# The lag stage of a four-part sequence kernel: query and key projected by halves, norms from transposed pair sums, the moves between partitions behind the rotation

## What is computed

```python
q, k, v = (causal_dwconv(silu(x @ W), conv_w) for each of Wq, Wk, Wv)   # 4 taps
z, a, b = x @ Wz, x @ Wa, x @ Wb
q = q * cos + rot_half(q) * sin      # rot_half(u): u1, u2 = halves of u; [-u2, u1]
k = k * cos + rot_half(k) * sin
q = q / max(norm(q), 1e-12);  k = k / max(norm(k), 1e-12)
for s in range(4):                   # k, v and a, delayed by s positions
    out += (sum(q * lag(k, s)) / sqrt(128) * sigmoid(lag(a, s) * b)) * lag(v, s)
out = out * rms(out) * norm_w * silu(z)
return out @ Wout
```

## Time and profile before

| | us |
|---|---|
| median of 3 runs | 3301.22 (3300.37 to 3301.49) |
| the profiled execution | 3301.86 |
| its span | 3300.1 |
| TensorE busy in the span | 3091.1 (94%), granted clock 0.966 on average |
| VectorE, ScalarE, GpSimd busy | 1793.2 (54%), 1160.3 (35%), 1041.8 (32%) |
| lag stage, about | 977 to 2160 |

### The profile page before, as it was taken

How to read it: one execution, slowest core, us unless ns; L and a number is a source line. 1 busy time by engine, 2 the same in 40 slices (tenths; PEclk the granted TensorE clock), 3 DMA queues, 4 the chain that set the end, 5 groups by cost and what they waited for, 6 DMA issues and landing times. The chain is left out here.

```text
span 3300.1 us, 39332 instructions
## 1 busy us (share of the span) xinstructions
PE 3091.1 (94%) x14752; PEld 2575.3 (78%) x14752; DVE 1793.2 (54%) x2587; ACT 1160.3 (35%) x2498; POOL 1041.8 (32%) x678
## 2 busy tenths in 40 slices
PE   6886499999979999999999999959999999999997
PEld 5665388888858888888888888848888888888886
DVE  4888633333367777777777777773222222222225
ACT  4232222112125555655555656532211121112110
POOL 4556223222224333333333333222222232223221
PEclk9987699999989999999999999979999999999999
DMA  3000101000032222222222222121010001000001
GB/s 116 1 1 0 61 20 39 20 20 1 1 110 59 58 61 58 62 58 62 74 60 60 61 59 61 40 77 58 20 39 20 19 20 39 20 20 27 12 0 51
DMA packets 54318, 135.46 MB, mean 41 GB/s; under 512 B 8305, under 2 KB 8689, under 8 KB 51313
## 3 DMA queue, kind: packets, MB, share of 16 engines
q1 hardware_dynamic: 54128, 132.95, 13.4%
HBM read 90.71 MB, written 8.65 MB: 30 GB/s over the span
## 5 line engine op out<-in xcount | busy, mean ns | idle before, releaser
L530 DVE TENSOR_TENSOR experts_inner<-experts_U,experts_gated 128x512 f32<-128x512 f32 x128 | 88.5, 691 | 593.5 <-PE experts_U L46 587.9
L492 POOL TENSOR_TENSOR experts_inlo<-experts_inner,experts_inhi 128x512 fp32r<-128x512 f32 x128 | 165.4, 1293 | 754.9 <-ACT experts_inhi L460 754.9
L543 DVE SCALAR_TENSOR_TENSOR x_tok<-experts_D,expert_weight,x_tok 128x512 f32<-128x512 f32 x256 | 191.3, 750 | 148.9 <-PE experts_D L46 148.9
L1437 DVE SCALAR_TENSOR_TENSOR lag_cq<-lag_A,lag_conv,lag_cq 128x511 f32<-128x511 f32 (+2 forms) x192 | 142.8, 744 | 196.0 <-ACT lag_cq L1349 196.0
L457 ACT ACTIVATE experts_gated<-experts_G 128x512 f32<-128x512 f32 x128 | 76.5, 598 | 458.5 <-PE experts_G L46 458.5
L1412 POOL TENSOR_TENSOR lag_rot_q<-lag_cq,lag_cos_sin 128x512 f32<-128x512 f32 x64 | 83.0, 1297 | 478.9 <-DVE lag_cq L1437 478.9
L44 PE MATMUL lag_A<-xT_hi,lag_w_hi 128*128 128x512 f32 x512 | 211.5, 413 | 3.8 <-DVE lag_cq L1437 2.7
L44 PE MATMUL lag_B<-xT_hi,lag_w_hi 128*128 128x512 f32 x512 | 212.6, 415 | 0.0
L460 ACT ACTIVATE experts_inhi<-experts_inner 128x512 fp32r<-128x512 f32 x128 | 80.9, 632 | 374.5 <-DVE experts_inner L530 374.5
L44 PE MATMUL experts_G<-xT_hi,experts_whi 128*128 128x512 f32 x528 | 207.4, 393 | 0.8 <-DVE expert_weight L1079 0.8
L45 PE MATMUL experts_G<-xT_lo,experts_whi 128*128 128x512 f32 x528 | 206.9, 392 | 0.0
(11 more groups left out here) (279 smaller groups left out, 8178.4 us busy)
## 6 DMA issues: line engine op xcount, KB each, us to landing
lag_raw<-in_head_weights SPq DMA_DIRECT2D x16, 1024.0 KB, 6.2
lag_b_row<-lag_b_scratch SPq DMA_DIRECT2D x64, 256.0 KB, 3.2
lag_swapped_q<-lag_cq SPq DMA_DIRECT2D x128, 128.0 KB, 2.3
lag_swapped_k<-lag_ck SPq DMA_DIRECT2D x128, 128.0 KB, 2.3
experts_raw<-in_expert_gate SPq DMA_DIRECT2D x16, 512.0 KB, 3.7
experts_raw<-in_expert_up SPq DMA_DIRECT2D x16, 512.0 KB, 4.6
experts_raw<-in_expert_down SPq DMA_DIRECT2D x16, 512.0 KB, 5.6
x_tok<-in_x SPq DMA_DIRECT2D x4, 1024.0 KB, 5.3
```

Source lines behind the costliest of these rows:

```text
L492: pool.tensor_tensor(in_lo[t % 2][:, f, :], inner[f][:, :], f32(in_hi[t % 2][:, f, :]), ALU.subtract).then_inc(s_hlo, 1)
L530: ins = dve.tensor_tensor(inner[f][:, :], U[f][:, :], gated[f][:, :], ALU.mult)
L543: ins = dve.scalar_tensor_tensor(row, D[tt][:, :], expert_weight[:, bass.ds(e + j * EXPERTS, 1)], row, op0=ALU.mult, op1=ALU.add)
L1437: dve.scalar_tensor_tensor(out[:, shift:], src[:, 0:SEQ - shift], wj, out[:, shift:], op0=ALU.mult, op1=ALU.add).then_inc(done, 1)
```

## The change

The halves of query and key are sorted anew on the host (`by_halves`): the first matrix of a head gives channels 0 to 63 of q and 0 to 63 of k (bank A, `c1`), the second the channels 64 to 127 of both (bank B, `c2`). The convolution weights follow. The partners of the rotation then lie on the same partition of two tiles: r1 = c1 cos - c2 sin, r2 = c2 cos + c1 sin. The results are moved by four DMAs into `rot_q` and `rot_k`, where all channels of q lie on one tile and all of k on another; before, it was the inputs that were moved.

The squares of `c1` and `c2` are added on GpSimd (`pairs`), transposed by TensorE into the second bank of the `scores` tile, and summed over each half by a reduction on VectorE, which gives eight sums (query and key, alternating by tile). On TensorE the second projection moves ahead of the scores. `gain` gets a second buffer, and VectorE takes `gain` before `prob`.

```diff
         squares, pairs = sb("squares", [P, 2, SEQ]), sb("pairs", [P, SEQ])
+        gain = [sb(f"gain{p}", [P, TPB, BAND]) for p in range(2)]
+        turned = scores[:, 2:4, :].rearrange("p a n -> p (a n)")
...
@@ SyncE @@
-                        sp.wait_ge(s_cq, f.s * TAPS + TAPS)
-                        until(sp, s_rot_q, f.s)
-                        for half in range(2):
-                            to, of = half * 64, 64 - half * 64
-                            sp.dma_start(swapped_q[to:to + 64, :], cq[of:of + 64, :]).then_inc(s_swap_q, 16)
...
+                        sp.wait_ge(s_r1, f.s + 1)
+                        until(sp, s_s, f.s)
+                        sp.dma_start(rot_q[0:64, 0:SEQ], r1[0:64, :]).then_inc(s_move1, 16)
+                        sp.dma_start(rot_k[0:64, :], r1[64:128, :]).then_inc(s_move1, 16)
+                        sp.wait_ge(s_r2, f.s + 1)
+                        sp.dma_start(rot_q[64:128, 0:SEQ], r2[0:64, :]).then_inc(s_move2, 16)
+                        sp.dma_start(rot_k[64:128, :], r2[64:128, :]).then_inc(s_move2, 16)
...
@@ TensorE @@
-                        projection(f, 0, A, s_q)
+                        projection(f, 0, A, s_a1)
+                        until(pe, s_sz, f.s - 1)
+                        projection(f, 1, B, s_a2)
                     if l1:
-                        pe.wait_ge(s_rot_q, l1.s + 1)
-                        pe.wait_ge(s_rot_k, l1.s + 1)
-                        pe.wait_ge(s_n2, l1.s + 1)
+                        pe.wait_ge(s_move1, l1.s * 32 + 32)
+                        pe.wait_ge(s_move2, l1.s * 32 + 32)
+                        pe.wait_ge(s_sum, l1.s + 1)
...
-                    if f:
-                        until(pe, s_sz, f.s - 1)
-                        projection(f, 1, B, s_k)
...
-                        pe.wait_ge(s_sqr, f.s * 2 + 2)
+                        pe.wait_ge(s_pair, f.s + 1)
                         until(pe, s_prob, f.s)
-                        for n in range(2):
-                            for t in range(TPB):
-                                col = NORM_AT + n * TPB + t
-                                last = pe.matmul(scores[:, 0, col:col + 1], squares[:, n, t * P:(t + 1) * P],
-                                                 ones[:, :], start=True, stop=True)
+                        for t in range(TPB):
+                            last = pe.transpose(turned[:, t * P:(t + 1) * P], pairs[:, t * P:(t + 1) * P], ident[:, :])
...
@@ GpSimd @@
                     if f:
-                        until(pool, s_s, f.s)
-                        pool.wait_ge(s_cq, f.s * TAPS + TAPS)
-                        pool.tensor_tensor(rot_q[:, 0:SEQ], cq[:, :], cos_sin[:, 0, :], ALU.mult).then_inc(s_cos_q, 1)
+                        pool.wait_ge(s_c1, f.s * TAPS + TAPS)
+                        until(pool, s_move1, f.s * 32)
+                        pool.tensor_tensor(r1[:, :], c1[:, :], cos_sin[:, 0, :], ALU.mult).then_inc(s_cos1, 1)
...
+                        pool.tensor_tensor(r2[:, :], c2[:, :], cos_sin[:, 0, :], ALU.mult).then_inc(s_cos2, 1)
+                        pool.wait_ge(s_sqr, f.s * 2 + 2)
+                        until(pool, s_nrm, f.s)
+                        pool.tensor_tensor(pairs[:, :], squares[:, 0, :], squares[:, 1, :], ALU.add).then_inc(s_pair, 1)
...
@@ VectorE @@
+                        tap(0, f, A, c1, 1, s_c1)
+                        dve.wait_ge(s_gate, f.s + 1)
+                        until(dve, s_prob, f.s - 1)
+                        dve.scalar_tensor_tensor(gain[f.s % 2][:, :, :], gate[:, :, :], 1.0,
+                                                 band_t[:, :].unsqueeze(1).to_broadcast([P, TPB, BAND]),
+                                                 op0=ALU.add, op1=ALU.mult).then_inc(s_gain, 1)
+                        tap(0, f, A, c1, 2, s_c1)
                     if l1:
                         dve.wait_ge(s_s, l1.s + 1)
                         dve.wait_ge(s_gain, l1.s + 1)
                         until(dve, s_o, l1.s)
+                        dve.tensor_tensor(prob[:, :, :], gain[l1.s % 2][:, :, :], scores[:, :, 0:BAND],
+                                          ALU.mult).then_inc(s_prob, 1)
                     if f:
+                        tap(0, f, A, c1, 3, s_c1)
+                        dve.wait_ge(s_t2, f.s + 1)
+                        tap(1, f, B, c2, 1, s_c2)
+                        dve.wait_ge(s_c1, f.s * TAPS + TAPS)
+                        until(dve, s_r2, f.s)
+                        dve.tensor_tensor(cross2[:, :], c1[:, :], cos_sin[:, 1, :], ALU.mult).then_inc(s_cross2, 1)
+                        tap(1, f, B, c2, 2, s_c2)
...
                         accumulate(l2, 0)
                     if f:
+                        tap(1, f, B, c2, 3, s_c2)
                     if l2:
                         accumulate(l2, 1)
                     if f:
+                        dve.wait_ge(s_c2, f.s * TAPS + TAPS)
+                        until(dve, s_r1, f.s)
+                        dve.tensor_tensor(cross1[:, :], c2[:, :], cos_sin[:, 1, :], ALU.mult).then_inc(s_cross1, 1)
                         dve.wait_ge(s_tv, f.s + 1)
                         tap(2, f, A, cv, 1, s_cv)
+                        dve.wait_ge(s_cos1, f.s + 1)
+                        dve.wait_ge(s_cross1, f.s + 1)
+                        dve.tensor_tensor(r1[:, :], r1[:, :], cross1[:, :], ALU.subtract).then_inc(s_r1, 1)
                         tap(2, f, A, cv, 2, s_cv)
+                        dve.wait_ge(s_cos2, f.s + 1)
+                        dve.wait_ge(s_cross2, f.s + 1)
+                        dve.tensor_tensor(r2[:, :], r2[:, :], cross2[:, :], ALU.add).then_inc(s_r2, 1)
                         tap(2, f, A, cv, 3, s_cv)
...
-                        dve.tensor_scalar(norm2[:, :], scores[:, 0, NORM_AT:NORM_AT + 2 * TPB], 1e-24, None,
-                                          ALU.max).then_inc(s_n2, 1)
+                        dve.tensor_reduce(norm2[:, :], turned.rearrange("p (a n) -> p a n", n=HDIM // 2), AX.X,
+                                          ALU.add).then_inc(s_sum, 1)
+                        dve.wait_ge(s_sum, f.s + 1)
+                        dve.tensor_scalar(norm2[:, :], norm2[:, :], 1e-24, None, ALU.max).then_inc(s_n2, 1)
...
@@ host @@
+    def by_halves(q, k):
+        both = np.stack([t.reshape(-1, HEADS, 2, HDIM // 2) for t in (q, k)], 3)
+        return [both[:, :, half].reshape(q.shape) for half in range(2)]
```

More of the change, by code:

```diff
@@ L1114, in lagged_attention @@
         wo_lo = [sb(f"wo_lo{p}", [P, HID], F32R) for p in range(2)]
-        cq, ck, cv = sb("cq", [P, SEQ]), sb("ck", [P, SEQ]), sb("cv", [P, SEQ])
-        swapped_q, swapped_k = sb("swapped_q", [P, SEQ]), sb("swapped_k", [P, SEQ])
+        c1, c2, cv = sb("c1", [P, SEQ]), sb("c2", [P, SEQ]), sb("cv", [P, SEQ])
+        cross1, cross2 = sb("cross1", [P, SEQ]), sb("cross2", [P, SEQ])
+        r1, r2 = sb("r1", [P, SEQ]), sb("r2", [P, SEQ])
         rot_q, rot_k = sb("rot_q", [P, SEQ + PAD]), sb("rot_k", [P, SEQ])
-        squares = sb("squares", [P, 2, SEQ])
+        squares, pairs = sb("squares", [P, 2, SEQ]), sb("pairs", [P, SEQ])
         b_row = sb("b_row", [P, SEQ + PAD])
-        gate, gain = sb("gate", [P, TPB, BAND]), sb("gain", [P, TPB, BAND])
+        gate = sb("gate", [P, TPB, BAND])
+        gain = [sb(f"gain{p}", [P, TPB, BAND]) for p in range(2)]
         prob = sb("prob", [P, TPB, BAND])
@@ L1136, in lagged_attention @@
         scores = bank("scores", (P, TPB, 256))
-        NORM_AT = 160
+        turned = scores[:, 2:4, :].rearrange("p a n -> p (a n)")
         T, O = bank("T"), bank("O")
         OP = [bank(f"OP{j}") for j in range(2)]
-        ahead = before(ctx, [t[:, :] for t in (swapped_q, swapped_k, cq, ck, zs, cv)], [wo_hi[1][:, :], wo_lo[1][:, :]],
+        ahead = before(ctx, [t[:, :] for t in (cross1, cross2, c1, c2, zs, cv)], [wo_hi[1][:, :], wo_lo[1][:, :]],
                        [t[:, :] for t in (T, O, *OP, A, B)])
@@ L1149, in lagged_attention @@
         s_whi, s_wlo = sem("whi"), sem("wlo")
[L1150 to L1159, removed]
+        s_a1, s_a2, s_v, s_z = sem("a1"), sem("a2"), sem("v"), sem("z")
+        s_s1, s_s2, s_sv, s_sz = sem("s1"), sem("s2"), sem("sv"), sem("sz")
+        s_t1, s_t2, s_tv = sem("t1"), sem("t2"), sem("tv")
+        s_c1, s_c2, s_cv = sem("c1"), sem("c2"), sem("cv")
+        s_cos1, s_cos2 = sem("cos1"), sem("cos2")
+        s_cross1, s_cross2 = sem("cross1"), sem("cross2")
+        s_r1, s_r2 = sem("r1"), sem("r2")
+        s_move1, s_move2 = sem("move1"), sem("move2")
+        s_sqr, s_pair = sem("sqr"), sem("pair")
+        s_nrm, s_sum, s_n2, s_rn = sem("nrm"), sem("sum"), sem("n2"), sem("rn")
         s_b, s_gate, s_gain = sem("b"), sem("gate"), sem("gain")
@@ L1443, in accumulate @@
                     until(dve, s_acc, st.s * TPB + t - 1)
-                    dve.scalar_tensor_tensor(row, OP[t % 2][:, :], at(rnorm[st.rbuf], t), row,
```

(22 more changed lines are left out.)

74 lines of the change are left out of this document (29 added, 45 removed).

## The result

Five runs of each kernel: 3317.78 us (3317.18 to 3323.58) against 3301.22 (3299.76 to 3303.93), a ratio of 1.0053 with a 95% interval of 1.004 to 1.0067. The change makes the kernel 16.6 us slower, 0.5%: small, but clear of the noise. The forecast was 3323.

A forecast was written before the change was run, and what follows sets the result against it. TensorE bounds the lag stage now (slot 18.36 us); after the change the round through the other engines does. 34 x 18.60 + 30 x 18.84 against 1175.0 gives +22.6, 3324, taken as 3323 us; range 3270 to 3346.

The forecast's parts named there:

- reduction to floor: VectorE's reduction of 512 elements, put at 0.69 us; the floor then follows 0.73 later than before.
- slot, plain / two splits: One pass of the lag stage's loop, without or with two GpSimd weight splits: 18.60 or 18.84 us, before 18.36.
- The two prices that the row at 1520.70 gave: VectorE/GpSimd contention: blocked GpSimd ends 1.17 us after VectorE's end; the next VectorE sum ends 0.54 after GpSimd's.
- TensorE's part: Norm matmuls of 1.71 us a slot become four transposes of 0.38; TensorE's work falls to 17.03, alone giving 85 us.
- The exclusion: VectorE and GpSimd both on two SBUF operands: the second waits; blocked VectorE instructions take 1.34, 1.34 and 1.05 us.
- the rule's 1.97: Blocked VectorE product's end after GpSimd's start by the skill's rule, 1.29 + 0.68 us; the forecast used 1.84.
- The round through values and SiLU: Loop through VectorE, GpSimd and ScalarE: values at 13.59 us hold ScalarE 1.05, SiLU at 14.64, next zero at 18.60.
- a smaller exclusion: VectorE/GpSimd rivals: no blocking, 3238 us, chance 0.10; half of it, 3258 to 3291 us, chance 0.14.
- a fall of the clock: Rival: TensorE's clock falls for its new idle time, 0.5 to 1 us a slot, 3350 to 3385; chance 0.05.
- The 0.3 us for TensorE's new order: Both projections ahead of the scores make `prob` and the value projection late: 5.3 against 5.0 us, slot 17.3.
- TensorE's idle time: Some 1.6 us a slot: 0.8 before the value projection, 0.3 before the `z` projection, the rest before `cv` transposes.
- The scores' wait for the moves at the end: At the stage's end no projection covers the four moves: about 1 us once, given back by the first slot's slack.

The follow-up runs named there:

- e9: e8 with the norms taken by TensorE again (16 passes of two columns; no pair sum, transposes or reduction): 3298.5 us.
- e8: The changed kernel with the edits of e1, e2, e5 and e7 together: 3226.9 us.
- e4: The changed kernel with GpSimd's two cosine products replaced by fills that read nothing, cosine part left out: 3239.5 us.
- e7: The changed kernel with sine products directly behind their taps, ahead of GpSimd's products, and the weights' low parts behind the power on GpSimd: 3256.0 us.
- e1: The changed kernel with ScalarE's values behind the first SiLU and `c1` copy, and the second SiLU and copy ahead of the weight splits: 3287.1 us.
- e6: The changed kernel with a second, unused reduction of the same 512 elements ahead of the used one: 3355.8 us.
- e10: e8 with the changed kernel's order on TensorE, both projections ahead of the scores: 3239.6 us.
- e5: The changed kernel with TensorE's order of before, the second projection behind the scores: 3319.8 us.
- e2: The changed kernel with the rotation's sums `r1` and `r2` behind the third tap of `cv` instead of between the taps: 3309.2 us.

## Why the prediction was right

The side, the mechanism and the size (+21.8 forecast from 3301.2, +16.6 measured) were right. Step by step, counted from the last `c1` tap (1503.72 in the rows above):

| step | forecast | measured |
|---|---|---|
| GpSimd's first product starts | 0.89 | 0.83 |
| `cross2` ends | 2.73 | 2.67 |
| `cross1` ends | 6.70 | 6.59 |
| `pairs` ends | 7.87 | 7.76 |
| `r1` ends | 8.41 | 8.31 |
| `y` | 10.25 | 10.15 |
| reduction to floor | 0.73 | 0.70 |
| SiLU | 14.64 | 14.51 |
| slot, plain / two splits | 18.60 / 18.84 | 18.49 / 18.76 |

The two prices that the row at 1520.70 gave came out as well: `pairs` ends 1.17 behind `cross1`, and `r1` 0.55 behind `pairs` (0.54 forecast). In that row VectorE was not the first on the scene, as the prediction reads it: a weight split was still running on GpSimd (1518.45 + 2.53 = 1520.98 in the earlier trace rows), which fits its 0.83 instead of 0.68.

- *TensorE's part.* The transposes take 0.36 as forecast (0.38). Of the 85 us that they would free, e9 shows 72, the difference between the norms by transposes and by matmuls when all else is alike; the long slots of e8 account for part of the rest.
- *The exclusion* was shown three ways: in the durations, in e4 (reads taken away, while two fills ran beside `cross1`) and in e7 (order of arrival turned round). The rule of the Trainium skill ("SBUF — State Buffer", section "Who interferes with whom") holds in kind, and also in that a GpSimd instruction that only writes does not contend, as far as e4 shows. In size the rows of before were the better guide: the blocked `cross2` ended 1.84 after GpSimd's start, to the hundredth, `cross1` 1.87 after it, and the rule's 1.97 would have put the sum at 3348.
- *The round through values and SiLU* was shown by e1, which cuts it, and e6, which lengthens it by a reduction's spacing (0.59 in its trace, 1511.89 to 1512.48) and finds 0.59 x 64.
- *The 0.1 a slot too much* (6 us) is mostly one term that enters twice: the reaction of GpSimd to the last tap of `c1` and of `c2`, 0.83 and 0.81 (1507.63 to 1508.44) and not 0.89. Another 0.03 lies in the reduction.
- *The rivals.* Neither a smaller exclusion nor a fall of the clock happened. The 0.3 us for TensorE's new order were right as a bound (17.3 without the round; e10 has 17.3) and rightly counted at nothing in the sum (e5).
- *TensorE's idle time.* By starts it is 0.76 ahead of the value projection, 0.18 ahead of the z projection and 0.46 ahead of the `cv` transposes, 1.4 in all; forecast were 0.8, 0.3 and the rest of 1.6.
- *What was off.* The scores' wait for the moves at the end was 1.61, not 1. Both sizes of e1 and e2 were missed: e1 because `prob` waits for the scores next, 0.28 a slot, e2 because three dependent taps back to back cost 0.08 each.

## What to carry to other kernels

An engine at 99% is the bound only as long as the round through the others is shorter: before relieving it, add up that round and compare it with the slot, since here 1.4 us of slack was all there was. Where GpSimd and VectorE both work on two SBUF operands, see to it that the engine with slack arrives second: here VectorE came 0.04 us ahead of GpSimd instead of 0.5 behind, and that was worth most of 62 us. And look in the program of each in-order engine for an instruction that waits for the end of one step and stands ahead of the start of the next: that is where a round can close. Here moving the values behind the SiLU left no work out and gained 31 us (e1).

## What the runs showed of the hardware

- What the engine that comes second pays depends on when it comes: VectorE's product took 1.35 when it came 0.49 behind GpSimd's, 1.65 when it came 0.20 behind, and 0.68 alone; GpSimd's took 1.81 when it came 0.04 behind VectorE's, and 1.30 unblocked.
- A GpSimd fill, which reads nothing, did not hold VectorE: 0.68 beside two of them (e4).
- A waiting VectorE instruction gets its turn between two GpSimd instructions that follow each other at once: with two splits behind the product, `cross2` still took 1.35, and the splits 2.98 together instead of 2.53.
- Three taps that each need the one ahead hold VectorE 2.22 us, 0.74 each, where unrelated instructions of this kind start 0.66 apart.
- TensorE kept its upper clock (granted 1.00 over the stretch) with 64 of 1175 us idle by its busy time, in pieces of 0.3 to 0.6 us in the slot shown.
